# A prologue rebuilt: the long convolution on x as it lies in memory, and weights split in place

## The chip, the cores and the metric

The program runs on one NeuronCore of a Trainium2 chip. The metric is the device time of one execution in microseconds. Three runs of the kernel before took 577.61, 577.98 and 578.83 us (median 577.98). TensorE does the matrix products, VectorE and ScalarE (DVE and ACT in the profile) the elementwise work, GpSimd (POOL) a third share of it; SyncE (SP) issues all the transfers, which run on 16 DMA engines.

## The reference

Two stages on x, of shape (64 batches, 32 channels, 512 positions), float32. The first is a long convolution per channel whose taps are computed from parameters, cut off at each batch's length:

```python
kernel = _get_kernel(log_dt, C, log_A_real, A_imag, Lq)     # (32, 512): a sum over 64 complex modes
y = irfft(rfft(u * mask) * rfft(kernel))[..., :Lq]          # causal convolution along the positions
y = (y + u * mask * D[:, None]) * mask                      # mask: position < length of the batch
x = x + y
```

The second is a gated network on rows of 512, with 64 batches x 32 channels = 2048 rows, an inner size of 1376, and a low-rank addition (rank 16, one of 16 tables chosen by the batch's index) on each of its three products:

```python
gate = x @ W_gate.T + 0.5 * (x @ A_gate[i].T) @ B_gate[i].T
up   = x @ W_up.T   + 0.5 * (x @ A_up[i].T)   @ B_up[i].T
act  = silu(gate) * up
x = x + act @ W_down.T + 0.5 * (act @ A_down[i].T) @ B_down[i].T
```

## The kernel before

The kernel has a prologue (the convolution, and the splitting of the weights) and then 16 tiles of 128 rows for the gated network. Every engine runs a list of instructions of its own, and the order is written out by hand: only semaphores tie the engines together, so an instruction that waits holds back everything behind it on its engine. That holds for SP too, whose list is the order in which transfers are issued.

*The tiles* (`body` on each engine) take each product as three passes in a short float32 form: a value is split into a high part (ScalarE copies it into the short form) and a low part (value less high part), and high*high, high*low and low*high are summed. A tile needs `w_hi`, `w_lo` (gate and up weights, in 12 pieces: 3 chunks of columns x 4 blocks of rows) and `wd_hi`, `wd_lo` (down weights, 6 pieces).

*The splitting of the weights.* SP loads a piece into one of three staging slots (`load_piece`, L226), ScalarE writes its high part (`split_hi`, L445), GpSimd subtracts to get the low part (`split_lo`, L393) and so frees the slot. The last down pieces are split during tile 0.

*The taps.* VectorE works out the parameters in a long chain of small dependent steps (L612 to L722, 128x32 values each), of which GpSimd turns one result into the exponents of all magnitudes (L407) and ScalarE takes their exponential in one instruction (L469). Then, for each of four groups of 8 channels, VectorE reduces phases (L645 to L656), ScalarE takes sines (L452 to L456), VectorE builds two tables (L739 to L747), TensorE multiplies them (L924, `taps`) and VectorE copies the result out (L727, L728). SP writes these taps to `kpad` in DRAM (`store_taps`, L239), where each channel has 128 zeros and then its 512 taps.

*The convolution* goes by 16 pairs of channels. x lies in SBUF with the position within a block of 128 on the partitions. For each pair SP reads from `kpad` a matrix `toep` of 128 rows x 2 channels x 512 values (`load_toep`, L247), in which row p is the row of taps that starts p+1 values into the channel. Rows that start later as p grows fit an input whose positions are reversed, and so each pair of x is also loaded a second time, reversed by the host: `um` from `xr` (`load_um`, L252). VectorE masks `um` (L755), TensorE does 8 products into PSUM (`conv`, L937), VectorE masks the result into `cv` (L759), and adds it to x (L765; GpSimd for the first four pairs, L400). There are four slots of `toep` and `um` (RC = 4); the load for pair p waits until pair p-4 has been convolved. After the last pair VectorE gathers the first tile's columns of x into `xt` (L810), TensorE starts the low-rank product on them (L967), the high and the low part of `xt` are made, and tile 0 begins.

The transfer on which `toep` rests reads, with one instruction, with these steps and counts (slowest first, in values of 4 bytes):

```python
src = bass.AP(tensor=kpad, offset=pair * (2 * (P + NL)) + 1, ap=[[1, P], [P + NL, 2], [1, NL]])
```

Of the kernel before, what the change touches and what calls it, by code (L numbers as in the profile page):

```python
# [14 lines left out]
F32 = mybir.dt.float32  # L15
# [5 lines left out]
P = 128  # L21
# [18 lines left out]
RS = 3  # L40
# [21 lines left out]
def program(nc, xT, xr, wgu, wd, atab, btab, prm, lens, idx, out):  # L62
    top = ExitStack()
    with top:
# [6 lines left out]
        kpad = nc.dram_tensor("kpad", (NH, P + NL), F32, kind="Internal")  # L71


        w_hi = sb(top, "w_hi", [P, KB, WG], F32R)
        w_lo = sb(top, "w_lo", [P, KB, WG], F32R)
        x = sb(top, "x", [P, NH, KB, NB])
        ident = sb(top, "ident", [P, P])
        amask = sb(top, "amask", [P, NH, BT])
# [4 lines left out]
        with ExitStack() as pk:  # L83
# [7 lines left out]
            prm_sb = sb(pk, "prm_sb", [P, N_PRM, NH])  # L91
# [3 lines left out]
            zeros = sb(pk, "zeros", [NH, P])  # L95
            k_sb = sb(pk, "k_sb", [PA, NG, HG, PB])

        wd_hi = sb(top, "wd_hi", [P, FB, NL + LR], F32R)
        wd_lo = sb(top, "wd_lo", [P, FB, NL + LR], F32R)
# [4 lines left out]
        b_raw = [sb(top, "b_raw0", [LR, 2 * 512])]  # L104


        with ExitStack() as pa:
            toep = sb(pa, "toep", [P, RC, 2, NL])
            um = sb(pa, "um", [P, RC, 2 * KB * NB])
            cv = sb(pa, "cv", [P, 2, 2 * KB * NB])  # L110
            len_i = sb(pa, "len_i", [P, NB], I32)
            len_f = sb(pa, "len_f", [P, NB])
            lcol = sb(pa, "lcol", [P, 2, KB])
            lmask = sb(pa, "lmask", [P, 2, KB, NB])
            stage = sb(pa, "stage", [P, RS, 2 * 512])


        b_raw.append(sb(top, "b_raw1", [LR, 2 * 512]))
# [5 lines left out]
        x_lo = sb(top, "x_lo", [P, 2, KB, P], F32R)  # L124
        h_act = sb(top, "h_act", [P, 2, 512])
# [22 lines left out]
        stage_in = [sem(f"stage_in{i}") for i in range(RS)]  # L148
        stage_hi, stage_lo = sem("stage_hi"), sem("stage_lo")
        consts, ident_s, amask_ok, amask_ps, amaskt_ok = (sem("consts"), sem("ident_s"), sem("amask_ok"), sem("amask_ps"),  # L150
                                                 sem("amaskt_ok"))
# [3 lines left out]
        logmag, mag_done, trig_in, trig_done = sem("logmag"), sem("mag_done"), sem("trig_in"), sem("trig_done")  # L155
# [4 lines left out]
        um_in = [sem(f"um_in{i}") for i in range(RC)]  # L160
        um_ready, conv_ps, conv_sb, x1_pool = sem("um_ready"), sem("conv_ps"), sem("conv_sb"), sem("x1_pool")
        x1_dve = sem("x1_dve")
# [38 lines left out]
        for c in range(NC):  # L201
            for kb in range(KB):
                cols = slice(chunk_col(c, 0), chunk_col(c, 0) + 2 * CH[c][1])
                pieces.append((wgu[kb * P:(kb + 1) * P, cols], w_hi[:, kb, cols], w_lo[:, kb, cols], P, (2 * CH[c][1],)))
        for f0 in range(0, FB - 1, 2):
            pieces.append((wd[f0 * P:(f0 + 2) * P, :].rearrange("(g p) n -> p g n", p=P),
                           wd_hi[:, f0:f0 + 2, 0:NL], wd_lo[:, f0:f0 + 2, 0:NL], P, (2, NL)))
        pieces.append((wd[(FB - 1) * P:NF, :], wd_hi[0:FLAST, FB - 1, 0:NL], wd_lo[0:FLAST, FB - 1, 0:NL], FLAST, (NL,)))

        NP_GU = KB * NC  # L210

        def staged(n):
            shape = pieces[n][4]
            size = shape[0] * (shape[1] if len(shape) > 1 else 1)
            v = stage[0:pieces[n][3], n % RS, 0:size]
            return v.rearrange("p (g n) -> p g n", g=2) if len(shape) > 1 else v
# [6 lines left out]
        def _(sp):  # L223
# [25 lines left out]
            def load_um(pair, slot, first):  # L249
                if not first:  # L250
                    sp.wait_ge(conv_ps, pair - RC + 1)
# [889 lines left out]
```

## Time and profile before

| | us |
|---|---|
| median of three runs | 577.98 |
| the profiled execution | 577.4 |
| its span, from the first to the last instruction | 575.5 |
| TensorE busy in the span | 518.0 |
| first product of pair 0 of the convolution | 45.23 |
| first product of tile 0 (low-rank, L967) | 101.66 |
| granted clock of TensorE over the span | 0.99 |

Times in the profile count from the start of the span. A group of instructions is named by line, engine, operation and the tensors it writes and reads; "x16" is the number of instructions. An idle time is put down to whatever ended it. In a window, the DMA share is the mean busy share of the 16 DMA engines (a little over 1 where packets overlap), and GB/s is what they moved together.

### The profile page before, as it was taken

The page shows a single profiled execution, that of the slowest core. Times are in us where ns is not written, and L with a number is a line of the kernel's source. Part 1 is how long each engine was busy: PE and PEld are TensorE (multiplying, and loading weights), DVE is VectorE, ACT ScalarE, POOL GpSimd, SP SyncE. Part 2 cuts the span into 40 slices and gives each one's busy share as a digit, 9 for nine tenths or more (in the row PEclk, how much of TensorE's full clock was granted, in tenths as well). Part 3 has the DMA queues.
Part 4 walks back from the last instruction along what each step waited for, and adds up shares of the span by engine and source line. Part 5 has one row for each costly group of instructions (what it writes and reads, how often), then busy time and mean ns, then how long its engine had stood idle before and what let it go on. Part 6 is the DMA issues. An engine that isn't in the chain of part 4 may idle for free.

```text
span 575.5 us, 10131 instructions
## 1 busy us (share of the span) xinstructions
PE 518.0 (90%) x3169; PEld 475.4 (83%) x3169; DVE 297.7 (52%) x577; ACT 194.3 (34%) x394; POOL 74.2 (13%) x74
## 2 busy tenths in 40 slices
PE   0007897999999999999999999999999999999997
PEld 0006887798989898989999999999999999998987
DVE  7989768874444444444353535353535353535342
ACT  3613101743333333333333324242423333333331
POOL 7434412640000000000000000000000000000000
PEclk9999999899999999999999999999999999999999
DMA  7626898730404040404040403030303030303000
GB/s 286 235 55 203 288 324 291 180 103 23 113 5 115 2 119 0 120 0 119 0 115 5 114 6 110 10 110 10 107 13 107 13 107 13 107 13 107 14 19 19
DMA packets 32307, 53.20 MB, mean 92 GB/s; under 512 B 7586, under 2 KB 16194, under 8 KB 32290
## 3 DMA queue, kind: packets, MB, share of 16 engines
q1 hardware_dynamic: 32290, 53.00, 31.3%
q8 instruction: 8, 0.13, 0.1%
q14 instruction: 9, 0.07, 0.1%
HBM read 48.69 MB, written 4.28 MB: 92 GB/s over the span
## 4 chain that ended last, share of the span: by engine, by line
PE 85%; DVE 11%; DMA 1%; issue 1%; POOL 1%; ACT 0%; DVEq 0%; SPq 0%; ACTq 0%
PE ps_u L989 21%; PE ps_g L989 20%; PE ps_db L1025 12%; PE ps_da L1025 12%; PE ps_x L1016 3%; PE ps_x L967 2%; PE ps_u L937 2%; PE ps_g L999 2%; PE ps_g L1000 2%; PE ps_u L1000 2%; PE ps_u L999 2%; PE ps_g L937 2%; PE ps_x L1054 1%; DMA um<-xr 1%; PE ps_da L1083 1%
## 5 line engine op out<-in xcount | busy, mean ns | idle before, releaser
L825 DVE TENSOR_TENSOR b_spl<-b_raw,b_spl 64x512 fp32r<-64x512 f32 (+1 forms) x96 | 66.6, 695 | 52.5 <-ACT b_spl L499 49.0
L499 ACT CAST b_spl<-b_raw 64x512 fp32r<-64x512 f32 (+1 forms) x96 | 54.6, 569 | 76.8 <-PE ps_u L1000 76.8
L989 PE MATMUL ps_g<-w_hi,x_hi 128*128 128x512 f32 (+1 forms) x192 | 72.8, 379 | 0.0
L989 PE MATMUL ps_g<-w_lo,x_hi 128*128 128x512 f32 (+1 forms) x192 | 71.1, 370 | 0.0
L989 PE MATMUL ps_g<-w_hi,x_lo 128*128 128x512 f32 (+1 forms) x192 | 71.0, 370 | 0.0
L989 PE MATMUL ps_u<-w_lo,x_hi 128*128 128x512 f32 (+1 forms) x192 | 70.7, 368 | 0.0
L989 PE MATMUL ps_u<-w_hi,x_hi 128*128 128x512 f32 (+1 forms) x192 | 70.6, 368 | 0.0
L989 PE MATMUL ps_u<-w_hi,x_lo 128*128 128x512 f32 (+1 forms) x192 | 70.5, 367 | 0.0
L434 POOL COPY xt<-x 128x512 f32 (+1 forms) x15 | 9.8, 653 | 394.5 <-PE ps_x L1054 390.9
L861 DVE TENSOR_TENSOR h_act<-h_act,ps_u 128x512 f32<-128x512 f32 (+1 forms) x48 | 30.4, 633 | 52.2 <-PE ps_u L1000 52.1
L1025 PE MATMUL ps_da<-wd_hi,ht_hi 128*128 128x288 f32 (+1 forms) x176 | 54.6, 310 | 0.0
L1025 PE MATMUL ps_db<-wd_hi,ht_hi 128*128 128x288 f32 (+1 forms) x176 | 53.2, 302 | 0.0
L1025 PE MATMUL ps_db<-wd_hi,ht_lo 128*128 128x288 f32 (+1 forms) x176 | 52.0, 296 | 0.0
L1025 PE MATMUL ps_db<-wd_lo,ht_hi 128*128 128x288 f32 (+1 forms) x176 | 51.9, 295 | 0.0
L1025 PE MATMUL ps_da<-wd_lo,ht_hi 128*128 128x288 f32 (+1 forms) x176 | 51.8, 294 | 0.0
L1025 PE MATMUL ps_da<-wd_hi,ht_lo 128*128 128x288 f32 (+1 forms) x176 | 51.7, 294 | 0.0
L518 ACT ACTIVATE h_act<-ps_g 128x512 f32<-128x512 f32 (+1 forms) x48 | 26.5, 552 | 63.9 <-PE ps_g L1000 63.9
L868 DVE TENSOR_TENSOR ht_lo<-ps_x,ht_hi 128x512 fp32r<-128x512 f32 (+1 forms) x48 | 28.9, 603 | 30.0 <-ACT ht_hi L534 28.3
L989 PEld LDWEIGHTS ps_g<-w_hi,x_lo 128*128 128x128 f32 x192 | 36.4, 189 | 5.4
L989 PEld LDWEIGHTS ps_u<-w_hi,x_hi 128*128 128x128 f32 x192 | 36.1, 188 | 5.2
L989 PEld LDWEIGHTS ps_u<-w_hi,x_lo 128*128 128x128 f32 x192 | 36.0, 188 | 5.1
L989 PEld LDWEIGHTS ps_u<-w_lo,x_hi 128*128 128x128 f32 x192 | 36.0, 188 | 5.1
(167 smaller groups left out, 986.6 us busy)
## 6 DMA issues: line engine op xcount, KB each, us to landing
a_raw<-atab SPq DMA_DIRECT2D x64, 152.0 KB, 2.4
toep<-kpad SPq DMA_DIRECT2D x16, 512.0 KB, 5.4
b_raw<-btab SPq DMA_DIRECT2D x128, 64.0 KB, 2.1
stage<-wgu SPq DMA_DIRECT2D x8, 512.0 KB, 5.0
um<-xr SPq DMA_DIRECT2D x16, 256.0 KB, 5.7
x<-xT SPq DMA_DIRECT2D x8, 512.0 KB, 6.7
out<-y_sb SPq DMA_DIRECT2D x15, 256.0 KB, 2.1
b_raw<-btab SPq DMA_DIRECT2D x64, 44.0 KB, 1.8
```

The lines of the kernel that those rows point to most:

```text
L499: nc.scalar.copy(b_spl[0:LR, up, 0:w], b_raw[slot][:, up * w:(up + 1) * w]).then_inc(b_hi, 1)
L518: nc.scalar.activation(h_act[:, s, 0:w], ps_g[s][:, 0:w], ACT.Silu).then_inc(silu_ok, 1)
L825: V.tensor_tensor(b_spl[LR:P, up, 0:w], b_raw[slot][:, up * w:(up + 1) * w], b_spl[0:LR, up, 0:w].bitcast(F32), ALU.subtract).then_inc(b_l ...
L861: V.tensor_tensor(h_act[:, s, 0:w], h_act[:, s, 0:w], ps_u[s][:, 0:w], ALU.mult).then_inc(act_ok, 1)
L868: V.tensor_tensor(ht_lo[:, f0:f0 + full, :], ps_x[bank][:, 0:full * P].rearrange("p (f t) -> p f t", t=P), ht_hi[:, f0:f0 + full, :].bitca ...
L937: last = T.matmul(ps_c[slot][:, at + d * NB:at + KB * NB], toep[:, slot, h, d * P:(d + 1) * P], um[:, slot, at:at + n], start=(d == 0), st ...
L967: ins = T.matmul(ps_x[0][:, 0:P], w, xt[:, kb, :], start=(kb == 0), stop=(kb == KB - 1))
L989: T.matmul(ps[:, 0:w], xs[:, q, kb, :], ws[:, kb, col:col + w], start=(kb == 0 and xs is x_hi and ws is w_hi), stop=False)
L999: T.matmul(ps[:, 0:w], t_hi[:, up, :], b_spl[:, up, 0:w], start=False, stop=False)
L1000: T.matmul(ps[:, 0:w], t_lo[:, up, :], b_spl[:, up, 0:w], start=False, stop=True).then_inc(u_ps if up else g_ps, 1)
L1016: ins = T.transpose(ps_x[bank][0:rows, f * P:(f + 1) * P], h_act[:, s, f * P:f * P + rows], ident[:, :])
L1025: ins = T.matmul(ps[:, 0:c1 - c0], hs[0:rows, f, :], ws[0:rows, f, c0:c1], start=(f == 0 and hs is ht_hi and ws is wd_hi), stop=(bank == 1 ...
```

## The change

- The convolution reads x as it lies. `um`, `xr`, `cv` and the masks on the input are gone. The rows of `toep` now start one value *earlier* as p grows, so the source of the load steps backwards. `kpad` holds two copies of all taps, each written by its own transfer; rows 0 to 63 of `toep` are read from the first copy and rows 64 to 127 from the second. So the source of a load has, slowest first, a step from one copy to the other (count 2), a step back by one value (count 64) and the 512 values of a row. A pair is loaded by two transfers, one for each channel.
- 1 is added to tap 0 besides D, so that the product is x plus the convolution, and one predicated copy per pair (`copy_predicated`, where the position is below the length) writes it from PSUM over x. VectorE does all 16 pairs. The input needs no mask, since the convolution is causal.
- Weights are loaded with no staging slots, straight to where their low part will be (`w_raw` and `w_lo` are the same memory). ScalarE writes the high part (`top_part`); the low part is subtracted in place (`rem_part`): gate and up pieces 0 to 7 by GpSimd, which begins only when all four tables are built (`tab_ready`), pieces 8 to 11 by VectorE behind pairs 10 to 13, and the 6 down pieces by VectorE in tile 0.
- SP issues all of x and then all 12 gate and up pieces before the first taps are stored. The down pieces go out one at a time behind the `toep` loads of pairs 10 to 15, and the first tile's low-rank tables behind those of pairs 8 and 9.
- The magnitudes are computed on ScalarE, 32 instructions of 128x48 with the exponent's factor as scale, in place of GpSimd's four and ScalarE's one.
- `take_x` gathers the first tile in two steps, the second for the last four channels only. `amask` is smaller; its transposed form is made before the convolution.

The core of the diff ("..." marks what is left out):

```diff
-        kpad = nc.dram_tensor("kpad", (NH, P + NL), F32, kind="Internal")
+        kpad = nc.dram_tensor("kpad", (2, NH, P + NL), F32, kind="Internal")
...
             def load_piece(n):
-                wait(sp, stage_lo, n - RS + 1)
-                sp.dma_start(staged(n), pieces[n][0]).then_inc(stage_in[n % RS], 16)
+                sp.dma_start(pieces[n][1], pieces[n][0]).then_inc(w_in[n], 16)
...
                 sp.wait_ge(k_ready, g + 1)
-                dst = bass.AP(tensor=kpad, offset=g * HG * (P + NL) + P, ap=[[PB, PA], [P + NL, HG], [1, PB]])
-                sp.dma_start(dst, k_sb[:, g, :, :]).then_inc(k_out[g], 16)
+                for i in range(2):
+                    dst = bass.AP(tensor=kpad, offset=(i * NH + g * HG) * (P + NL) + P,
+                                  ap=[[PB, PA], [P + NL, HG], [1, PB]])
+                    sp.dma_start(dst, k_sb[:, g, :, :]).then_inc(k_out[g], 16)
 
             def load_toep(pair, slot, group, first):
 
-                sp.wait_ge(k_out[group], 16)
+                sp.wait_ge(k_out[group], 32)
                 if not first:
                     sp.wait_ge(conv_ps, pair - RC + 1)
-                src = bass.AP(tensor=kpad, offset=pair * (2 * (P + NL)) + 1, ap=[[1, P], [P + NL, 2], [1, NL]])
-                sp.dma_start(toep[:, slot, :, :], src).then_inc(toep_in[slot], 16)
...
+                for h in range(2):
+                    src = bass.AP(tensor=kpad, offset=(2 * pair + h) * (P + NL) + P,
+                                  ap=[[NH * (P + NL) - P // 2, 2], [-1, P // 2], [1, NL]])
+                    sp.dma_start(toep[:, slot, h, :], src).then_inc(toep_in[slot], 16)
...
+            for g in range(NG):
+                load_x(g, 0)
+                load_x(g, 1)
+            for n in range(NP_GU):
+                load_piece(n)
...
+            sp.wait_ge(zero_out, 32)
             store_taps(0)
             for pair in range(RC):
                 load_toep(pair, pair, 0, True)
             store_taps(1)
+            load_toep(RC, 0, 1, False)
             store_taps(2)
+            load_toep(RC + 1, 1, 1, False)
+            store_taps(3)
+            load_toep(RC + 2, 2, 1, False)
+            load_toep(RC + 3, 3, 1, False)
...
+            for pair in range(2 * RC, PAIRS):
+                load_toep(pair, pair % RC, pair // RC, False)
+                if pair == 2 * RC:
+                    load_a(0, 0, ids0)
+                if pair == 2 * RC + 1:
+                    load_b(0, 0, 0, ids0)
+                if pair >= 2 * RC + 2:
+                    load_piece(NP_GU + pair - (2 * RC + 2))
...
+            def rem_part(n):
+                pool.wait_ge(w_top, n + 1)
+                nc.gpsimd.tensor_tensor(pieces[n][3], pieces[n][1], pieces[n][2].bitcast(F32),
+                                        ALU.subtract).then_inc(w_rem_pool, 1)
...
+            pool.wait_ge(tab_ready, 2 * NG)
+            for n in range(KB):
+                rem_part(n)
             pool.wait_ge(a_in, 16 * BT)
             pack_a(0)
-            for n in range(10, len(pieces)):
-                split_lo(n)
+            for n in range(KB, NP_POOL):
+                rem_part(n)
...
+            def magnitudes(g):
+                for h in range(g * HG, (g + 1) * HG):
+                    ins = nc.scalar.activation(gg[:, g, h - g * HG, :], lvec[:, :], ACT.Exp, scale=small[:, DAR, h:h + 1])
+                ins.then_inc(mag_done, 1)
...
-            def mask_output(pair, slot):
+            def add_conv(pair):
+
                 dve.wait_ge(conv_ps, pair + 1)
-                V.tensor_tensor(two(cv[:, slot % 2, :]), two(ps_c[slot][:, :]), mask_out, ALU.mult).then_inc(conv_sb, 1)
...
+                V.copy_predicated(x[:, 2 * pair:2 * pair + 2, :, :].rearrange("p h k b -> p h (k b)"),
+                                  lmask[:, :, :].rearrange("p k b -> p (k b)").unsqueeze(1).broadcast_to([P, 2, KB * NB]),
+                                  ps_c[pair % RC][:, :].rearrange("p (h n) -> p h n", h=2)).then_inc(x1_ok, 1)
...
             taps(3)
...
+            for pair in range(1, PAIRS - 2):
+                add_conv(pair)
+                if pair >= PAIRS - 6:
+                    rem_part(NP_POOL + pair - (PAIRS - 6))
+            dve.wait_ge(x1_ok, PAIRS - 2)
+            take_x(0, NH - 4).then_inc(xt_ok, 1)
+            add_conv(PAIRS - 2)
+            add_conv(PAIRS - 1)
+            dve.wait_ge(x1_ok, PAIRS)
+            take_x(NH - 4, NH).then_inc(xt_ok, 1)
...
+            def conv(pair):
+                slot = pair % RC
+                pe.wait_ge(toep_in[slot], 32 * (pair // RC) + 32)
+                pe.wait_ge(x_in[2 * pair // HG], 32)
+                wait(pe, x1_ok, pair - RC + 1)
```

TensorE's order is as before: taps(0), conv(0), taps(1), conv(1) to conv(3), taps(2), conv(4), taps(3), and then the other pairs.

## Rows read from the trace of the kernel before

**Rows 1.** The page: busy time by engine, and the chain's shares.

```profile
PE 518.0 (90%) x3169; PEld 475.4 (83%) x3169; DVE 297.7 (52%) x577; ACT 194.3 (34%) x394; POOL 74.2 (13%) x74
...
PE 85%; DVE 11%; DMA 1%; issue 1%; POOL 1%; ACT 0%; DVEq 0%; SPq 0%; ACTq 0%
```

**Rows 2.** Timeline of PE: start us, us, what [idle before <- who ended it].

```profile
45.23 4.95 PE L937 MATMUL ps_g<-um,toep 128*128 128x256 f32 x16 [6.92 <-DMA toep<-kpad]
77.42 4.98 PE L937 MATMUL ps_g<-um,toep 128*128 128x256 f32 x32
92.30 5.00 PE L937 MATMUL ps_u<-um,toep 128*128 128x256 f32 x32 [0.21 <-issue]
101.66 2.08 PE L967 MATMUL ps_x<-xt,a_gu 128*128 128x128 f32 x8 [4.17 <-DVE amask_t L813]
107.89 0.50 PE L999 MATMUL ps_g<-b_spl,t_hi 128*128 128x512 f32 x1 [0.27 <-DVE t_lo L851]
```

**Rows 3.** Timeline of VectorE, the chain of parameters.

```profile
5.38 3.64 DVE L620 SCALAR_TENSOR_TENSOR small<-small 128x64 f32<-128x64 f32 x6
10.84 0.80 DVE L678 TENSOR_SCALAR small<-small 128x32 f32<-128x32 f32 x1
14.02 2.32 DVE L682 SCALAR_TENSOR_TENSOR small<-small 128x32 f32<-128x32 f32 x1
26.79 2.29 DVE L714 TENSOR_TENSOR small<-prm_sb,small 128x32 f32<-128x32 f32 x1
33.71 0.19 DVE L717 TENSOR_TENSOR small<-prm_sb,small 128x32 f32<-128x32 f32 x1
38.66 0.16 DVE L728 TENSOR_TENSOR k_sb<-k_sb,prm_sb 1x8 f32<-1x8 f32 x1
```

**Rows 4.** Timeline of GpSimd.

```profile
26.68 6.94 POOL L393 TENSOR_TENSOR w_lo<-stage,w_hi 128x1024 fp32r<-128x1024 f32 x3 [7.68 <-ACT w_hi L445]
```

**Rows 5.** Windows: PE, PEld, DVE, ACT, POOL busy, granted clock, DMA share, GB/s.

```profile
0.00:5.00 5.00, 0.00 (x0) 0.00 (x0) 2.15 (x8) 1.28 (x1) 3.49 (x17) 1.00 0.59 169
5.00:10.00 5.00, 0.00 (x0) 0.00 (x0) 4.66 (x13) 2.36 (x3) 2.70 (x2) 1.00 0.76 293
8.00:20.00 12.00, 0.00 (x0) 0.00 (x0) 11.90 (x23) 1.93 (x2) 10.30 (x7) 1.00 1.02 392
75.00:95.00 20.00, 19.79 (x130) 18.83 (x131) 15.62 (x26) 0.00 (x0) 0.00 (x0) 1.00 1.01 337
```

**Rows 6.** The `toep` loads by their line: time to landing.

```profile
L247 SPq DMA_DIRECT2D toep<-kpad x16: 370/377/593, 40.4 to 87.3; - x16
...
DMA to landing us min/median/max: 4.0/5.4/8.9
```

**Rows 7.** The stores of taps by their line.

```profile
L239 SPq DMA_DIRECT2D kpad<-k_sb x4: 337/387/432, 38.9 to 70.7; - x4
...
DMA to landing us min/median/max: 1.5/2.7/4.6
```

**Rows 8.** VectorE by line, 60 to 101 us: count | busy, mean ns.

```profile
L755 DVE TENSOR_TENSOR um<-um,lmask 128x512 f32<-128x512 f32 x12 | 8.3, 690 | 5.9 <-DMA um<-xr 5.9
L759 DVE TENSOR_TENSOR cv<-ps_u,lmask 128x512 f32<-128x512 f32 x8 | 5.4, 680 | 0.0
L765 DVE TENSOR_TENSOR x<-x,cv 128x512 f32<-128x512 f32 x4 | 3.7, 920 | 0.1
L810 DVE COPY xt<-x 128x512 f32<-128x512 f32 x1 | 1.8, 1774 | 0.0
```

**Rows 9.** Timelines of ScalarE (sine, high parts) and VectorE (low parts).

```profile
20.42 0.23 ACT L464 ACTIVATE small<-small 128x32 f32<-128x32 f32 x1
101.66 0.62 ACT L491 CAST x_hi<-xt 128x512 fp32r<-128x512 f32 x1 [3.22 <-DVE xt L810]
103.04 1.29 DVE L825 TENSOR_TENSOR b_spl<-b_raw,b_spl 64x512 fp32r<-64x512 f32 x2
105.32 0.30 ACT L508 CAST t_hi<-t_m 64x128 fp32r<-64x128 f32 x1
```

More of the change, by code:

```diff
@@ L39 @@
 DB_W = NL - DA_W
-RS = 3
 RC = 4
@@ L94, in program @@
             half_pi = sb(pk, "half_pi", [P, 1])
-            zeros = sb(pk, "zeros", [NH, P])
-            k_sb = sb(pk, "k_sb", [PA, NG, HG, PB])
         wd_hi = sb(top, "wd_hi", [P, FB, NL + LR], F32R)
+        with ExitStack() as landing:
+            wd_raw = sb(landing, "wd_raw", [P, FB, NL + LR])
         wd_lo = sb(top, "wd_lo", [P, FB, NL + LR], F32R)
@@ L124, in program @@
         x_lo = sb(top, "x_lo", [P, 2, KB, P], F32R)
+        with ExitStack() as pa:
+            with ExitStack() as pz:
+                zeros = sb(pz, "zeros", [NH, P])
+            toep = sb(pa, "toep", [P, RC, 2, NL])
+            len_i = sb(pa, "len_i", [P, NB], I32)
+            len_f = sb(pa, "len_f", [P, NB])
+            lcol = sb(pa, "lcol", [P, KB])
+            lmask = sb(pa, "lmask", [P, KB, NB], I32)
+            prm_sb = sb(pa, "prm_sb", [P, N_PRM, NH])
+            k_sb = sb(pa, "k_sb", [PA, NG, HG, PB])
         h_act = sb(top, "h_act", [P, 2, 512])
@@ L396, in add_conv @@
-            def add_conv(pair):
-                pool.wait_ge(conv_sb, pair + 1)
-                v = x[:, 2 * pair:2 * pair + 2, :, :].rearrange("p h k b -> p (h k b)")
-                nc.gpsimd.tensor_tensor(v, v, cv[:, pair % 2, :], ALU.add).then_inc(x1_pool, 1)
-            split_lo(0)
-            pool.wait_ge(consts, 6)
-            pool.wait_ge(dar_ok, 1)
-            for g in range(NG):
-                shape = [P, HG, PA + PB]
-                nc.gpsimd.tensor_tensor(gg[:, g], small[:, DAR, g * HG:(g + 1) * HG].unsqueeze(2).broadcast_to(shape),
-                                        lvec[:, :].unsqueeze(1).broadcast_to(shape), ALU.mult).then_inc(logmag, 1)
@@ L457, in trig @@
                                      scale=-1.0).then_inc(trig_done, 1)
-            for n in range(RS):
-                split_hi(n)
-            act.wait_ge(consts, 6)
+            act.wait_ge(amask_ok, 5)
+            nc.scalar.copy(amask_w[:, :, :], amask[0:LR, :].unsqueeze(1).broadcast_to([LR, NH, BT])).then_inc(amaskw_ok, 1)
+            act.wait_ge(consts, 5)
             act.wait_ge(ang_in, 1)
@@ L521, in ht_hi_part @@
                     act.wait_ge(ht_ps, NC * t + c + 1)
-                    if c == 0 and first:
-                        act.wait_ge(stage_lo, len(pieces))
-                    elif c == 0:
-                        act.wait_ge(down_ps, t)
+                    if c == 0:
+                        wait(act, down_ps, t)
                     f0, nf = BLK[c]
@@ L579, in _ @@
             b_hi_part(0, 0, 0, 1)
-            split_hi(NP_GU)
             tiles(act, body)
```

298 lines of the change are left out of this document (93 added, 205 removed).

## The prediction

> **What bounds the kernel now.** I read the page first: TensorE is busy for 518.0 of 575.5 us and has 85% of the chain that ended last, VectorE 11% [rows 1]. The timeline of TensorE says where the rest lies. Tile 0 starts at 101.66 and from 107.89 on the products run with no gap, so the tiles are bound by TensorE, and nothing of the change touches tiles 1 to 15. What the change can move is the point at which the first L999 runs, 107.89 [rows 2]. Everything before it is a chain of three parts:
>
> 1. VectorE's parameters, up to the first taps at 38.66 + 0.16 = 38.8 [rows 3].
> 2. Store and load: pair 0's product starts at 45.23, after TensorE has idled 6.92 us for `toep` [rows 2].
> 3. Sixteen pairs, 45.23 to 97.3. At full clock a pair takes 4.98 / 2 = 2.49 us, a first one after idling 4.95 [rows 2]. Then the tail, 97.3 to 107.89: 10.6 us.
>
> **Part 1, the parameters: -15.6 us.** VectorE's small operations take about 0.2 us (L717: 0.19) [rows 3], but 2.3 us where GpSimd is splitting weights: L714 starts at 26.79 and takes 2.29, within GpSimd's three subtractions from 26.68 to 33.62 [rows 3, 4]. So one operation of VectorE waits for one of GpSimd's, each time. The change leaves GpSimd idle until all tables are built. What goes: L620's six, 3.64 - 6 x 0.24 = 2.2; beside GpSimd's exponents L678 to L680 and L645, four times 0.80 - 0.18 = 2.5; L682 and L684, 2 x 2.1 = 4.3; L714 to L716, 3 x 2.1 = 6.3; of the lost mask instructions about 0.3. Sum 15.6, first taps at 23.2. The magnitudes on ScalarE are 32 instructions, each between 0.13 (starts apart) and 0.23 us (L464) [rows 9], 4 to 7 us in all, of which tables(0) needs 8: hidden beside VectorE's 9 us from the sines to table 0. Without that cover they would cost 2 us.
>
> **Part 2, what now lies ahead of the first store.** SP issues 0.1 MB of parameters, 4.19 MB of x and 5.64 MB of weights before it. The first ten microseconds moved 5 x 169 + 5 x 293 = 2.3 MB, and after that 392 GB/s are reached [rows 5]: the remaining 7.6 MB take 19.4 us, to 29.4. The store is issued at 23.3 and lands behind them, about 31.5 (the landing is 1.5 to 4.6 us when a queue is short [rows 7]), so 6 of the 15.6 us are given back. The first `toep` load is at the engines at 32.5. Doubled store and zeros cost 0.4 us of SP each and are in this.
>
> **Part 3, the loads of `toep`, the term that decides.** No row of before shows such a transfer. All bulk loads of before count 32 or more in the slowest step on both sides (`toep`: 128 rows). The new source counts 2 in its slowest step, then 64 backwards; the two halves can't be joined into one step. If the 16 engines get equal parts of the slowest step, only two parts can be given out. The bounds:
>
> - Below: a full-width load, 4.0 us to land, 5.4 in the median [rows 6]. Two loads a pair cost SP 0.37 us more, hidden in 2.49.
> - Above: two engines do all of it. In the stretch at 392 GB/s and share 1.02 one engine moves 392 / 16 / 1.02 = 24.0 GB/s; in the stretch of `toep` loads 337 / 16 / 1.01 = 20.9 [rows 5]. A load of 256 KB is 131,072 bytes an engine, 5.46 us at 24.0, and a pair takes 10.9 us instead of 2.49.
>
> I take the upper end and 24.0: a second copy of the taps makes sense only if the slowest step is the copy, and then this step is what a transfer is cut along; the other 14 engines would not be there to crowd the same rows of DRAM, which speaks for 24.0 and against 20.9.
>
> The Trainium skill says it outright (DMA: Bandwidth & Descriptors, section Why a DMA increments its semaphore by 16 and not by 1): a transfer issued by SP runs on the largest number of engines up to 16 that divides the count of the slowest step on both sides, here 2. No run here shows it yet. By the same page's 27 GiB/s an engine a pair would take 9.0 us, and the time would be some 670, an estimate.
>
> The sum for the upper end: four pairs of loads from 32.5, 43.7 us, to 76.2. The second store of taps (issued at about 50) has its share on the two busy engines and lands only behind them, so the fifth load is issued late: 2.5 us. Twelve pairs, 131.0 us, to 209.7. In between, the two engines also carry a sixteenth each of 3.5 MB (first tables and five down pieces), 0.22 MB, 9.1 us: to 218.8. Stores 3 and 4 find loads queued and add nothing. Pair 15's product runs on a TensorE that has idled, 4.95 us [rows 2]: the convolution ends at 223.8, where before it was 97.3.
>
> **Masks and adds.** Three passes of 0.68 to 0.92 us a pair (L755, L759, L765) become one predicated copy [rows 8]. Its price is not in the trace: between 0.68 and the three it replaces, 2.3. I take 0.7. Both ends are under 2.49 us a pair, so this is worth nothing until the last pair.
>
> **Weights.** The 18 high parts stay on ScalarE, with nothing behind them that is due. GpSimd's eight subtractions (6.94 / 3 = 2.3 us each [rows 4]) begin after table 3 and end before the last pair in either case. Four on VectorE behind pairs 10 to 13, about 0.9 us each (two inputs in SBUF, 704 long, by L765's 0.68 at 512), fit in a pair's 2.49. In tile 0, six take VectorE 1.3 us at most; they stand ahead of low parts that TensorE needs 6 and 12 us after 107.89, with 2 us to spare, and GpSimd no longer holds VectorE there. Nothing either way; without that slack, up to 2 us. The x loads that now all come first feed conv with no wait.
>
> **The tail: -3.7 us.** Before, from 97.3, the last mask (0.68), the last add and the gather run, the last two held up by GpSimd (1.77 for the gather, and the add's mean is 0.92 against 0.68 undisturbed [rows 8]); the low-rank product starts at 101.66. After: predicated copy 0.7, small gather 0.3, `x_hi` 0.62, `x_lo` 0.69, two low parts 1.29, the mask's copy 0.21 and t_m 0.29, four `t_hi` at 0.31 and four `t_lo` at 0.30 [rows 9], waits 0.4: 6.9 instead of 10.6. The last down piece lands before it.
>
> **The sum.** First L999 at 223.8 + 6.9 = 230.7, which is 122.8 later than 107.89. The profiled execution took 577.4 us (span 575.5), which becomes 700.2; the median of the runs stands 0.6 above that execution, so 701. By the bounds of the engine's rate: at 20.9 the loads and the rest take 27 more, 728; at 26 (the same share at the best) 14 less, 687. Start of the loads, bubbles and landings between pairs may be off by 10 either way, and a latency of 1 us exposed in each of 16 pairs would add 16. Own range 665 to 745.
>
> **The rivals.**
>
> - *Full width after all.* If the engines are dealt the rows whatever the outermost count is, pair 0 starts at 32.5 + 4.0 = 36.5, 8.7 us earlier. Then 16 pairs as before, about 52 us: the first is cold (4.95), pairs 5 and 6 wait for stores 3 and 4, which SP has ahead of their loads; from pair 10 on, 1.05 MB a pair at 337 GB/s take 3.1 us and slip by 1.5 in all behind four slots. End 90, tail 6.9: L999 at 96.9, 11 us earlier, time 566 to 567, within 556 to 574. For it: every load of before lands in 4.0 to 8.9 us [rows 6]. Against it: none of them had this shape. This is the rival on the other side; it decides where the last pair ends before 97.3 + 3.7 = 101.0, so where a pair's loads take less than (101.0 - 4.95 - 2.5 - 32.5) / 16 = 3.8 us, which is 138 GB/s, or between five and six engines at 24.0.
> - *Partial width.* A cut over four engines (say, over both steps in part) gives 5.46 us a pair: 32.5 + 87.4 + 2.5 + 4.6 + 2.5 + 6.9 = 136.4, 28.5 later, 606.
> - *Full width, but late landings.* Loads that land at 8.9 instead of 4.0 us [rows 6] for the three that TensorE waits for in the open (pairs 0, 5, 6) cost 14.7, and pairs 10 to 15 at 3.1 us another 4: 566.5 + 18.7 = 585, slower by 7.
>
> **How the numbers follow.** Two engines 0.77, full width 0.16, four engines or so 0.04, late landings 0.03. The predicted time is the first's, 701. Its own range of 665 to 745 holds 0.75, so the range goes down to the third case, 604 to 745. A measurement of this kernel can tell 0.2% from no change. Faster: the second case, 0.17 with what late landings leave; within 0.2%: 0.02; slower 0.81.
>
> **What the profile would show.** First `k_sb` sum at 23 us instead of 38.7, no VectorE operation of 2.3 us before it; pair 0's product at 43 to 46 in the narrow case (36 to 38 in the wide one), then TensorE idle until `toep` lands in most pairs, starts 10 to 12 us apart; DMA share near 2/16 and about 50 GB/s between 40 and 210 us; in TensorE's clock a long cold stretch; the tiles unchanged behind it. `toep` loads landing in 4 to 6 us with TensorE dense from 37 us on would prove me wrong at once, and so would a DMA share near 1 in that stretch.

## The result: 22% slower, and the profile after

The changed kernel takes 703.11 us (median of four runs, 703.03 to 703.19) against 578.11 us (four runs, 577.61 to 578.83): 1.2167 times as long, 95% interval 1.2145 to 1.2189. 701 us had been forecast. The profiled execution took 703.17 us, its span is 701.0.

The page after: busy time, two rows of the 40 slices of the span (TensorE's granted clock in tenths, and what the DMA engines moved), and the chain's shares.

```profile
PE 551.4 (79%) x3169; PEld 499.9 (71%) x3169; DVE 257.0 (37%) x556; ACT 200.4 (29%) x426; POOL 39.5 (6%) x55
...
PEclk9995556655567999999999999999999999999999
...
GB/s 315 266 47 51 41 52 50 92 76 101 75 90 39 81 12 100 41 59 88 10 98 31 67 87 11 98 22 76 81 17 97 16 84 77 22 95 12 89 15 16
...
PE 68%; SPq 19%; DMA 7%; DVE 3%; issue 1%; ACT 0%; DVEq 0%
```

TensorE had 85% of the chain [rows 1] and has 68%; SP's queue, absent before, has 19%. From the third slice (35 us on) 315 GB/s have become about 50, and 75 to 101 in the slices from 123 us on, where tables and down pieces are loaded beside `toep`. From the fourth slice to the twelfth (53 to 210 us) the clock stands at 0.5 to 0.6, near its lower level of 1.2 GHz. TensorE's product count is the same; it is busy 33 us longer, mostly since a pair's products take up to 4.96 us at the lower clock, against 2.49 [rows 2].

The timeline of TensorE: start, duration, what, and in brackets the idle time before it and who ended it.

```profile
44.21 4.51 PE L866 MATMUL ps_g<-x,toep 128*128 128x256 f32 x16 [22.07 <-DMA toep<-kpad]
55.32 4.08 PE L866 MATMUL ps_g<-x,toep 128*128 128x256 f32 x16 [5.99 <-DMA toep<-kpad]
65.75 4.96 PE L866 MATMUL ps_u<-x,toep 128*128 128x256 f32 x16 [6.35 <-DMA toep<-kpad]
76.22 4.96 PE L866 MATMUL ps_u<-x,toep 128*128 128x256 f32 x16 [5.51 <-DMA toep<-kpad]
90.35 4.95 PE L866 MATMUL ps_g<-x,toep 128*128 128x256 f32 x16 [8.21 <-DMA toep<-kpad]
...
205.16 4.26 PE L866 MATMUL ps_u<-x,toep 128*128 128x256 f32 x16 [7.19 <-DMA toep<-kpad]
217.81 4.75 PE L866 MATMUL ps_u<-x,toep 128*128 128x256 f32 x16 [8.39 <-DMA toep<-kpad]
...
229.31 0.50 PE L924 MATMUL ps_g<-b_spl,t_hi 128*128 128x512 f32 x1 [1.22 <-DVE t_lo L769]
```

Read the starts: 44.21, 55.32, 65.75, 76.22. A pair comes every 10.5 us, and each time TensorE has been idle for a `toep` load. L924 answers to L999 of before [rows 2] and starts at 229.31 instead of 107.89: 121.4 us later. The span grew by 125.5. So 121.4 us of the loss lie ahead of this row, and 4.1 behind it.

The windows (engines' busy time, granted clock, DMA share, GB/s) show the loads:

```profile
8.00:20.00 12.00, 0.00 (x0) 0.00 (x0) 10.87 (x58) 10.45 (x33) 0.00 (x0) 1.00 1.03 413
20.00:30.00 10.00, 1.04 (x16) 0.93 (x16) 8.39 (x21) 7.49 (x17) 0.00 (x0) 1.00 0.92 351
40.00:45.00 5.00, 0.79 (x2) 0.70 (x3) 0.00 (x0) 0.00 (x0) 0.00 (x0) 1.00 0.13 51
45.00:80.00 35.00, 17.15 (x76) 15.38 (x75) 5.37 (x14) 8.65 (x12) 0.00 (x0) 0.64 0.13 47
```

A share of 0.13 is 2 of 16 engines. A pair is 524,288 bytes, 262,144 for each of two engines, in 10.5 us: 25.0 GB/s an engine. The row of before for the stretch in which `toep` is loaded has share 1.01 and 337 GB/s [rows 5].

VectorE's first steps and its last ones ahead of tile 0, and the timeline of SP's queue:

```profile
4.50 1.52 DVE L563 SCALAR_TENSOR_TENSOR small<-small 128x64 f32<-128x64 f32 x6
16.98 0.19 DVE L656 TENSOR_TENSOR small<-prm_sb,small 128x32 f32<-128x32 f32 x1
22.49 0.16 DVE L670 SCALAR_TENSOR_TENSOR k_sb<-k_sb,prm_sb 1x8 f32<-1x8 f32 x1
...
222.59 0.72 DVE L696 COPY_PREDICATED x<-lmask,ps_u 128x512 f32<-128x512 int32 x1 [12.41 <-PE ps_u L866]
223.35 0.19 DVE L706 COPY xt<-x 128x64 f32<-128x64 f32 x1
```

```profile
22.73 0.84 SPq L235 DMA_DIRECT2D kpad<-k_sb  x2
30.29 31.89 SPq L245 DMA_DIRECT2D toep<-kpad  x8
62.22 6.29 SPq L235 DMA_DIRECT2D kpad<-k_sb  x2
```

The first taps are there at 22.65 (before 38.8 [rows 3]), and L563's six take 1.52 instead of 3.64. The store is issued at once, but the first `toep` load only at 30.29. Before, 1.6 us lay between taps and load (38.8 to 40.4 [rows 3, 6]), now 7.6: of the 16 us won, 6 are given back behind the weights.

### The profile page after: what moved, and what is told of

It is laid out like the page before. It is cut to its first block, busy times and chain, and to the rows that moved or that the text cites. A ratio compares the mean times of both kernels' runs of the same rounds, so it can differ in the third digit from the quotient of the medians.

```text
span 701.0 us, 10101 instructions
## 1 busy us (share of the span) xinstructions
PE 551.4 (79%) x3169; PEld 499.9 (71%) x3169; DVE 257.0 (37%) x556; ACT 200.4 (29%) x426; POOL 39.5 (6%) x55
## 4 chain that ended last, share of the span: by engine, by line
PE 68%; SPq 19%; DMA 7%; DVE 3%; issue 1%; ACT 0%; DVEq 0%
PE ps_u L914 17%; PE ps_g L914 17%; SPq L245 13%; PE ps_db L952 10%; PE ps_da L952 10%; DMA toep<-kpad 5%; SPq L220 4%; PE ps_x L943 3%; DMA kpad<-k_sb 2%; PE ps_x L893 2%; PE ps_g L924 1%; PE ps_u L924 1%; PE ps_u L925 1%; PE ps_g L925 1%; PE ps_x L981 1%; SPq L257 1%
## 5 line engine op out<-in xcount | busy, mean ns | idle before, releaser
L866 PE MATMUL ps_g<-x,toep 128*128 128x256 f32 (+3 forms) x128 | 37.5, 482 | 69.7 <-DMA toep<-kpad 69.7
L866 PEld LDWEIGHTS ps_g<-x,toep 128*128 128x128 f32 x128 | 33.4, 316 | 73.5 <-DMA toep<-kpad 70.7
L743 DVE TENSOR_TENSOR b_spl<-b_raw,b_spl 64x512 fp32r<-64x512 f32 (+1 forms) x96 | 60.4, 630 | 53.1 <-ACT b_spl L454 49.4
L866 PE MATMUL ps_u<-x,toep 128*128 128x256 f32 (+3 forms) x128 | 38.3, 489 | 52.5 <-DMA toep<-kpad 52.5
L866 PEld LDWEIGHTS ps_u<-x,toep 128*128 128x128 f32 x128 | 34.1, 322 | 56.7 <-DMA toep<-kpad 53.9
L952 PE MATMUL ps_da<-wd_hi,ht_hi 128*128 128x288 f32 (+1 forms) x176 | 54.6, 310 | 0.0
L952 PE MATMUL ps_db<-wd_hi,ht_hi 128*128 128x288 f32 (+1 forms) x176 | 53.3, 303 | 0.0
L952 PE MATMUL ps_db<-wd_lo,ht_hi 128*128 128x288 f32 (+1 forms) x176 | 52.0, 295 | 0.0
L952 PE MATMUL ps_db<-wd_hi,ht_lo 128*128 128x288 f32 (+1 forms) x176 | 51.9, 295 | 0.0
L952 PE MATMUL ps_da<-wd_lo,ht_hi 128*128 128x288 f32 (+1 forms) x176 | 51.8, 294 | 0.0
L952 PE MATMUL ps_da<-wd_hi,ht_lo 128*128 128x288 f32 (+1 forms) x176 | 51.6, 293 | 0.0
L398 ACT CAST wd_hi<-wd_raw 128x1024 fp32r<-128x1024 f32 (+1 forms) x6 | 5.8, 973 | 151.6 <-DMA wd_raw<-wd 151.6
```

The lines of the kernel that those rows point to most:

```text
L743: V.tensor_tensor(b_spl[LR:P, up, 0:w], b_raw[slot][:, up * w:(up + 1) * w], b_spl[0:LR, up, 0:w].bitcast(F32), ALU.subtract).then_inc(b_l ...
L866: last = T.matmul(ps_c[slot][:, at + d * NB:at + KB * NB], toep[:, slot, h, d * P:(d + 1) * P], v, start=(d == 0), stop=(d == KB - 1))
L952: ins = T.matmul(ps[:, 0:c1 - c0], hs[0:rows, f, :], ws[0:rows, f, c0:c1], start=(f == 0 and hs is ht_hi and ws is wd_hi), stop=(bank == 1 ...
```

## The experiments

**How wide is a load?** The theory on test is that the slowest step of the source, with count 2, is what a transfer is cut along. Then 4, 8 and 16 copies of the taps give 4, 8 and 16 engines. All three start from the changed kernel. The edit for 4:

```diff
-        kpad = nc.dram_tensor("kpad", (2, NH, P + NL), F32, kind="Internal")
+        kpad = nc.dram_tensor("kpad", (4, NH, P + NL), F32, kind="Internal")
...
-                for i in range(2):
+                for i in range(4):
...
-                                  ap=[[NH * (P + NL) - P // 2, 2], [-1, P // 2], [1, NL]])
+                                  ap=[[NH * (P + NL) - P // 4, 4], [-1, P // 4], [1, NL]])
```

Four copies:

> Four copies of the taps instead of two, so that the slowest step of a load's source counts 4 (32 rows backwards in each); two more stores a group. Theory of width (a load runs on as many engines as that count, 25 GB/s each): 512 KB on 4 engines is 5.2 us a pair instead of 10.5, DMA share about 0.25 in the stretch of the loads, time about 610 us. Rival theory of issue (SP spends 3.6 to 6.6 us on the issue of each backwards load, and that sets the pace): a pair still takes 10 us or more, time 701 to 710. Rival theory of backwards rows (DRAM or engines are slow when rows go down): no change either, 701 to 710.

Eight copies:

> Eight copies: the slowest step counts 8, eight stores a group. Width: 2.6 us a pair, about what TensorE takes (2.49); first store 2.4 us later, two later stores exposed by as much; time about 571 (564 to 582). Issue or backwards rows: 705 or more.

Sixteen copies:

> Sixteen copies: the slowest step counts 16, sixteen stores a group of 0.4 us of SP each. Width: loads of 256 KB land in 4 to 5 us, TensorE paces the pairs, but each group's store holds SP for 6.4 us, three of them in the open; time about 581 (572 to 592). Issue or backwards rows: 710 or more.

Measured: 630.82 us with four copies (ratio to the kernel before 1.0926, interval 1.0878 to 1.0975), 600.63 with eight (1.0404, 1.0362 to 1.0445), 601.49 with sixteen (1.0419, 1.0368 to 1.0469). One window of each (last two columns: share and GB/s), first four copies while little but `toep` is loaded, with two starts from TensorE's timeline:

```profile
41.00:60.00 19.00, 14.04 (x74) 12.78 (x75) 5.38 (x14) 8.65 (x12) 0.00 (x0) 0.93 0.26 88
```

```profile
51.57 2.62 PE L866 MATMUL ps_u<-x,toep 128*128 128x256 f32 x16 [1.94 <-DMA toep<-kpad]
57.10 4.29 PE L866 MATMUL ps_u<-x,toep 128*128 128x256 f32 x16 [2.91 <-DMA toep<-kpad]
```

Then eight copies, while nothing but `toep` is loaded, and sixteen, beside the down pieces, with the first store in SP's queue:

```profile
40.00:46.00 6.00, 4.65 (x16) 4.29 (x16) 0.00 (x0) 0.00 (x0) 0.00 (x0) 1.00 0.52 201
```

```profile
95.00:115.00 20.00, 14.51 (x94) 13.39 (x92) 8.23 (x12) 4.18 (x4) 8.02 (x4) 1.00 1.06 269
```

```profile
26.11 13.62 SPq L235 DMA_DIRECT2D kpad<-k_sb  x16
```

Share 0.13 with two copies, 0.26 with four, 0.52 with eight, 1.06 with sixteen: the width is the count of copies. With four, 5.5 us lie between the two pairs above, where it was 10.5.

All three times missed my numbers on the slow side, by 20 to 30 us. Two reasons hold for all of them. The first is the stores: SP issues every copy of every group by itself, 13.62 us for the first sixteen (9.40 for the first eight), with the loads queued behind, so that pair 0 starts at 46.33 with sixteen copies and 41.35 with eight, against 44.21 with two, and the later groups' stores stand ahead of loads too. The second is the down pieces, which take their part of the same engines: beside them the late pairs were 7 us apart with four copies, where I had taken 5.2, and 4.8 us with eight, where I had taken 2.6. With sixteen copies the rate comes on top: all engines are busy (1.06) but move 269 GB/s where the kernel before moves 337 [rows 5]. Eight copies show no such loss, with 201 / 16 / 0.52 = 24 GB/s an engine. So more copies recovered most of the loss, and none of the three kernels recovered all of it.

**Is it the 269 GB/s of an unlucky distance between the copies?** Copies of 81,920 bytes, an even distance; one spare channel makes it 84,480.

```diff
-        kpad = nc.dram_tensor("kpad", (16, NH, P + NL), F32, kind="Internal")
+        kpad = nc.dram_tensor("kpad", (16, NH + 1, P + NL), F32, kind="Internal")
```

> c16_sixteen_copies with each copy of the taps 2,560 bytes further on in DRAM (pitch 84,480 instead of 81,920 bytes). There 16 engines at a share of 1.05 moved only 268 GB/s, where the kernel before moved 337 at 1.01. If the pitch of the copies makes the engines meet in DRAM: above 320 GB/s at the same share and a time 5 us or more lower, about 595. If it is the cut of the rows over the engines (eight neighbouring rows each) or the step backwards: 260 to 275 GB/s and 600 to 602.

Measured: 599.55 us in a single run, and 251 GB/s at share 0.93 from 95 to 118 us. Divided by its share, that is 270 GB/s; by the same measure it is 254 at the even distance (269 / 1.06) and 334 in the kernel before (337 / 1.01). The distance is not what costs the most of it.

**Is it the width alone, or going backwards, or the rest of the rebuild?** The kernel before, with forward sources as ever, gets two copies and two loads a pair, once with the slowest step of 2, once with 128 rows as the slowest step:

```diff
-                src = bass.AP(tensor=kpad, offset=pair * (2 * (P + NL)) + 1, ap=[[1, P], [P + NL, 2], [1, NL]])
-                sp.dma_start(toep[:, slot, :, :], src).then_inc(toep_in[slot], 16)
+                for h in range(2):
+                    src = bass.AP(tensor=kpad, offset=(2 * pair + h) * (P + NL) + 1,
+                                  ap=[[NH * (P + NL) + P // 2, 2], [1, P // 2], [1, NL]])
+                    sp.dma_start(toep[:, slot, h, :], src).then_inc(toep_in[slot], 16)
```

In the control, the middle of the three reads `ap=[[1, P], [1, NL]]`, and all else is the same. The narrow one:

> The kernel before with one thing changed: two copies of the taps, two loads a pair, each with a source of 2 x 64 rows x 512 that goes forwards. Width: the rebuilt prologue has no part in it, a pair takes 10.5 us plus the two engines' share of the reversed x and the weights, and the time goes to about 716 (700 to 735). Backwards rows: forwards is what it was, 578 to 584. Issue (if it is the backwards step that makes the issue slow): 578 to 584 as well.

The control:

> Control for b2: the kernel before with two copies stored and two loads a pair, as there, but each load with 128 rows in its slowest step (from the first copy alone). Width: all that b2 lost comes back, 578 to 583 (two more stores, 16 more loads on SP, the last two behind nothing). If it was the doubling of stores and loads that cost b2 its 140 us: 700 or more.

Measured: 718.34 us narrow (ratio 1.2442, 1.2392 to 1.2493), 578.19 for the control (1.0004, 0.9979 to 1.0028). TensorE in the narrow one, and a window of the control:

```profile
65.97 4.80 PE L942 MATMUL ps_g<-um,toep 128*128 128x256 f32 x16 [5.05 <-DMA toep<-kpad]
77.55 4.14 PE L942 MATMUL ps_u<-um,toep 128*128 128x256 f32 x16 [6.79 <-DMA toep<-kpad]
```

```profile
75.00:95.00 20.00, 19.71 (x132) 18.77 (x131) 15.06 (x25) 0.00 (x0) 0.00 (x0) 1.00 0.96 331
```

11.6 us a pair in the old kernel, read forwards. This is the cleanest of the comparisons: the two differ in one access pattern, and the whole loss is there. It needs no backwards step and nothing of the rebuild, and two copies with two transfers a pair cost nothing by themselves.

A third variant of the kernel before asks why sixteen copies move only 269 GB/s; it reads forwards with `[NH * (P + NL) + P // 16, 16], [1, P // 16]`:

> The kernel before with sixteen copies of the taps, two loads a pair, each load of 16 x 8 rows x 512 forwards, eight neighbouring rows an engine. It tells apart why c16_sixteen_copies moved only 268 GB/s at a DMA share of 1.05. If it is the cut (eight neighbouring rows an engine): the stretch of the last eight pairs moves 260 to 290 GB/s at a share near 1, and a packet of 2 KB takes about 126 ns in the mean. If it is the step backwards: 330 GB/s or more there, as in the kernel before (337 at 1.01, 100 ns a packet). Sixteen stores a group cost about 6 us of SP each, three of them in the open, so the time is 590 to 610 either way.

Measured: 613.27 us in a single run. The last 15 us in which `toep` is loaded:

```profile
115.00:130.00 15.00, 14.12 (x88) 13.20 (x88) 9.04 (x15) 0.00 (x0) 0.00 (x0) 0.97 1.07 286
```

286 GB/s at share 1.07 are 267 by the measure above, with single stretches of 5 us between 263 and 320 GB/s. The mean lies in the range that was written down for the cut (260 to 290). A packet of 2,048 bytes (`toep` and `um` together) took 125.2 ns in the mean of this stretch, against 99.7 in the kernel before (75 to 95 us) and 126.5 with sixteen copies read backwards (95 to 115 us). That is what the cut was expected to show, too. So the direction is not what lowers the rate. It is the cut into 16 groups of 8 neighbouring rows, or the reading from 16 copies that comes with it; these two were not separated, and why they cost is open.

**Could SP's issue be the limit?** In the trace after, SP's queue is held for long at each load. By this line's summary (least, median, most, in ns) against 370/377/593 [rows 6]:

```profile
L245 SPq DMA_DIRECT2D toep<-kpad x32: 497/3620/6566, 30.3 to 197.5; - x32
```

If issuing were the limit, a second issuer would help. The loads of the odd channels go to ScalarE:

```diff
+            def load_second(pair):
+                slot = pair % RC
+                act.wait_ge(k_out[pair // RC], 32)
+                if pair >= RC:
+                    act.wait_ge(conv_ps, pair - RC + 1)
...
+                act.dma_start(toep[:, slot, 1, :], src).then_inc(toep_in[slot], 16)
```

> The changed kernel, with the load of each pair's second channel issued by ScalarE instead of SP; shapes as they are (slowest step counts 2). Width: both issuers give their loads to the same two engines, a pair takes 10.5 us as before, DMA share stays at 0.13, time 695 to 705. Issue (SP's 3.6 to 6.6 us a load are its own work, not a wait for the two engines): a pair takes 5.3 us, time about 620.

Measured: 700.51 us (ratio 1.2100, 1.2031 to 1.2170), where the changed kernel has 1.2167. The window from 55 to 77 us:

```profile
55.00:77.00 22.00, 11.04 (x35) 9.77 (x36) 1.15 (x4) 1.21 (x4) 0.00 (x0) 0.50 0.14 48
```

Still two engines, still 48 GB/s, from two queues. The 3.6 us in SP's queue are back-pressure, an effect and not the cause.

**What is the rest of the change worth?** The changed kernel with the old, forward load of a full pair. It needs the reversed input, so `um` is loaded again, but not masked; everything else of the change stays. Its queue order: four pieces ahead of the first store, the others among the loads.

```diff
+                src = bass.AP(tensor=kpad, offset=pair * (2 * (P + NL)) + 1, ap=[[1, P], [P + NL, 2], [1, NL]])
+                sp.dma_start(toep[:, slot, :, :], src).then_inc(toep_in[slot], 16)
+                if not first:
+                    load_um(pair)
```

> The rest of the change with the loads of the kernel before: one copy of the taps, one load a pair with 128 rows forwards, and x a second time with positions reversed as TensorE's input, unmasked; the predicated copy, the weights in place, the magnitudes and the tail as in the change; loads of weights spread over the convolution. If the width of the loads is all that is wrong with the change: first taps at 22.7, pair 0 at about 29.5, pairs as before (50 to 52 us), tail 6.8 us: first L999-like product at 88, time about 558 (552 to 566). If the predicated copy, the late low parts or the tail cost something that the narrow loads hid: 570 or more.

Measured: 574.05 us (ratio 0.9899, 0.9847 to 0.9950); I had expected 558. In the profiled execution, the slowest of the four at 575.96 us, pair 0 starts at 28.24, 17 us earlier than before, yet the first L938 (L999 of before) only at 101.71. Three windows show where the lead went:

```profile
50.00:55.00 5.00, 1.82 (x7) 1.61 (x6) 4.80 (x6) 0.00 (x0) 4.74 (x3) 0.50 0.27 29
60.00:65.00 5.00, 5.00 (x35) 4.72 (x33) 1.47 (x2) 1.56 (x2) 0.00 (x0) 1.00 1.05 374
80.00:85.00 5.00, 3.94 (x26) 3.54 (x25) 2.12 (x4) 2.09 (x2) 0.00 (x0) 1.00 1.05 387
```

The engines stand nearly idle at 50 us (29 GB/s), while SP waits to store taps that don't exist yet with loads queued behind, and from 60 us on they are full. If the DMA engines are the bound of the prologue once the parameters are short, a hole in their work is paid for at the end.

So the same kernel with its queue filled: the pieces that fit go ahead of the stores that wait, and four down pieces (not in these lines) go behind all `toep` loads.

```diff
             store_taps(1)
-            load_piece(6)
             load_toep(RC, 0, 1, False)
-            load_piece(7)
+            load_piece(6)
             load_toep(RC + 1, 1, 1, False)
-            store_taps(2)
+            load_piece(7)
             load_piece(8)
             load_toep(RC + 2, 2, 1, False)
-            store_taps(3)
             load_piece(9)
+            store_taps(2)
             load_toep(RC + 3, 3, 1, False)
             load_piece(10)
+            load_piece(11)
+            store_taps(3)
```

> hk_forward_loads with another order of transfers: pieces 6 to 11 issued ahead of stores 2 and 3, so that the engines have work while SP waits for taps, and only two down pieces ahead of the last pair, the other four behind it, split in tile 0 as in the kernel before. If the bytes ahead of the last pair bound hk_forward_loads (its engines stood at 0.27 of their time in 50 to 55 us and at 1.05 from 60 to 85): 2 MB less there and no hole, about 10 us earlier, 562 (557 to 568). If it is the chain of waits from store 3 to pair 7: 570 to 574.

Measured: 563.64 us (ratio 0.9757, 0.9713 to 0.9801), as expected (562). From 50 to 85 us, and the row that sets the start of the dense part:

```profile
50.00:85.00 35.00, 29.95 (x176) 27.87 (x175) 12.35 (x19) 5.83 (x8) 14.28 (x7) 0.91 1.00 331
```

```profile
89.34 0.50 PE L947 MATMUL ps_g<-b_spl,t_hi 128*128 128x512 f32 x1 [1.22 <-DVE t_lo L792]
```

No hole is left, and the tiles become dense at 89.34 instead of 101.71 (107.89 in the kernel before). Two things changed together, though. The four down pieces that went behind the loads are 1.77 MB, some 5 us at the 374 GB/s above (an estimate), and the rest of the 12.4 us is what filling the hole is worth. The two were not run one by one. The time lies where the bytes ahead of the last pair had put it, and clear of the 570 to 574 of a chain of waits.

**Does it matter that GpSimd waits for the tables?** In the kernel with forward loads, that one wait is gone:

```diff
-            pool.wait_ge(tab_ready, 2 * NG)
```

> As hk_forward_loads, but GpSimd subtracts as soon as a high part is there and does not wait for the tables. If GpSimd's subtractions hold VectorE by up to 2.3 us each, as they did in the kernel before, tables 1 to 3 come later and with them pairs 4 to 8: 2 to 6 us slower than hk_forward_loads, with VectorE operations of 2.3 us in its trace. If VectorE has slack there: the same within 1 us.

Measured: 577.02 us (ratio 0.9984, 0.9959 to 1.0009), 3.0 us slower than with the wait, within what was expected. The size is less sure than the sign: the four runs with the wait spread from 571.06 to 575.96 us, and the two profiled executions differ by 0.5. VectorE's last step of the first taps, and its second product of table 1, without the wait:

```profile
22.48 0.16 DVE L681 SCALAR_TENSOR_TENSOR k_sb<-k_sb,prm_sb 1x8 f32<-1x8 f32 x1
31.35 2.58 DVE L699 TENSOR_TENSOR e<-e,small 128x256 f32<-128x256 f32 x1
```

The same product with the wait:

```profile
29.15 0.42 DVE L700 TENSOR_TENSOR e<-e,small 128x256 f32<-128x256 f32 x1
```

GpSimd was subtracting from 28.79 to 38.6 in the first, and taps(1) came at 39.14 instead of 33.12. So the wait keeps table 1 short. It is not what shortened the parameters: the first taps are there at 22.64 without it too, because a subtraction needs a high part, and ScalarE writes its first one only at 27.66, behind the sines and the magnitudes. In the kernel before, GpSimd already subtracted at 6.59, 13.54 and 26.68 and raised the magnitudes' exponents from 9.65, in the middle of VectorE's chain.

**Why do the tiles take longer?** The 4 us behind L924 are in no step of the prediction. The tiles' period can be read from one row per tile, the low-rank product. Tile 1's and tile 15's are 14 periods apart. The changed kernel:

```profile
252.18 1.05 PE L893 MATMUL ps_x<-xt,a_gu 128*128 128x128 f32 x8
...
664.06 1.05 PE L893 MATMUL ps_x<-xt,a_gu 128*128 128x128 f32 x8
```

The kernel before, tile 1 and tile 11, ten periods:

```profile
130.52 1.05 PE L967 MATMUL ps_x<-xt,a_gu 128*128 128x128 f32 x8
...
422.36 1.05 PE L967 MATMUL ps_x<-xt,a_gu 128*128 128x128 f32 x8
```

411.88 / 14 = 29.42 us against 291.84 / 10 = 29.18. The kernels with eight copies and with the filled queue, both made from the changed one, have 29.42 too; the control made from the kernel before has 29.2. The difference is in the products of 512 columns. Here are the first and the twelfth of a row of twelve in tile 1, changed kernel first:

```profile
258.84 0.40 PE L914 MATMUL ps_u<-w_hi,x_hi 128*128 128x512 f32 x1
...
261.41 0.40 PE L914 MATMUL ps_u<-w_hi,x_lo 128*128 128x512 f32 x1
```

```profile
137.13 0.39 PE L989 MATMUL ps_u<-w_hi,x_hi 128*128 128x512 f32 x1
...
139.62 0.39 PE L989 MATMUL ps_u<-w_hi,x_lo 128*128 128x512 f32 x1
```

Eleven steps take 2.57 us against 2.49. In the mean of all 16 tiles one step takes 0.233 us against 0.228, and a tile has 48 of these products: 0.005 x 48 = 0.24 us, the whole difference of the period.

TensorE's instructions in a tile are the same. What differs is where the tensors lie: `amask` shrank from 512 bytes a partition to 16, beside a new `amask_w` of 512, and all that is allocated behind them (`x_hi`, `x_lo`, `b_spl`, `wd` and so on, but not `w_hi` and `w_lo`) sits 32 bytes further on. By the declarations, with the 16 bytes rounded up to 32, that is 32 more than a multiple of 64 where before it was a multiple of 64; no trace prints the addresses. In the kernel with the filled queue, one declaration moves to the end, which gives all these tensors the addresses of before:

```diff
-        amask = sb(top, "amask", [P, BT])
         amask_w = sb(top, "amask_w", [LR, NH, BT])
...
         ht_lo = sb(top, "ht_lo", [P, FB, P], F32R)
+        amask = sb(top, "amask", [P, BT])
```

> The kernel of the filled queue (563.64 us, ratio 0.9757, span 561.7), with one declaration moved: in all rebuilt kernels the mask tensor `amask` takes 16 bytes a partition where the kernel before gives it 512, beside `amask_w` of 512, and every tensor allocated behind it (wd, a_gu, b_spl, x_hi, x_lo, t_hi, ht_hi and so on) lies 32 bytes off the 64-byte boundary that it had before. Here `amask` is declared last, so that all tensors of the tiles lie at exactly the addresses of the kernel before; not one instruction differs. The question is the one step of the prediction that failed, the tiles unchanged: a tile takes 29.42 us in the changed kernel and all its relatives, 29.2 in the kernel before and in the two kernels built on it, and a 512-column product starts 0.233 us after the one before it against 0.227. Theory A, addresses: the tile's period goes back to 29.2, the products to 0.227, and the time falls by 15 to 16 tiles x 0.23 = 3.5 us, to 560 (559 to 561.5), ratio 0.969. Theory B, not the addresses (the instruction stream itself, since the tiles' operations in place or on another engine differ): the period stays at 29.42 and the time at 563 to 564.5, ratio 0.975. A value between says that both play a part.

Measured: 560.81 us (five runs, 559.08 to 561.68; ratio 0.9697, 0.9671 to 0.9723), and the period:

```profile
112.29 1.05 PE L916 MATMUL ps_x<-xt,a_gu 128*128 128x128 f32 x8
...
521.01 1.05 PE L916 MATMUL ps_x<-xt,a_gu 128*128 128x128 f32 x8
```

408.72 / 14 = 29.19. The steps between the products are back at 0.228 us in the mean. The period shows the effect more sharply than the two times do, since their intervals overlap. It was the addresses: not one instruction differs between these two kernels. Which tensor's it was is not separated. This version beats both kernels: 17 us less than before, by 18.3 us in the prologue (first L947 at 89.58) less 1.5 behind it.

## Why the prediction was right, and its one wrong step

- **The width of the loads** decided everything, and it was as forecast: two engines, by share 0.13, at 25.0 GB/s an engine (24.0 taken), a pair in 10.5 us alone (10.9) and 12.2 beside the down pieces (156.75 to 217.81 over five pairs). The long stretch at the lower clock came with it, as nine of the 40 slices show. The Trainium skill's rule (DMA: Bandwidth & Descriptors, section Why a DMA increments its semaphore by 16 and not by 1) gives a transfer of SP the largest number of engines up to 16 that divides the slowest count on both sides. The traces agree at 2, 4, 8 and 16 (shares 0.13, 0.26, 0.52, 1.06).
- **The parameters**: taps at 22.65, forecast 23.2. L563 to L670 show no 2-us holds. The reason given was half right: VectorE is free because GpSimd is idle, but it is not the wait for the tables that idles it here. Without that wait the first taps come at 22.64 as well, and the holds return only in table 1. By the traces it is that the exponents left GpSimd and that ScalarE's high parts come later; no run separates the two.
- **What lies ahead of the first store**: pair 0 at 44.21, forecast 32.5 + 10.9 = 43.4. That close a hit is in part luck. The first load was issued at 30.29, earlier than the 32.5 taken (DMA moved 413 GB/s from 8 to 20 us, 392 taken), and pair 0 then took 13.9 us and not 10.9. From 30 to 32 us the engines moved 6 GB/s; what held the first load is open.
- **The second store behind the narrow loads**: forecast 2.5 us. Pair 4 came 14.13 us after pair 3, 3.6 more than 10.5.
- **Predicated copy**: 0.72, forecast 0.7. **Tail**: from 222.56, where pair 15's product ends, to 229.31, 6.75 us, forecast 6.9; before it was 10.6. L924 at 229.31, forecast 230.7.
- **The wrong step: "nothing of the change touches tiles 1 to 15".** They took 0.24 us more each, 3.3 us over 14 periods; the rest of the 4 us lies in tile 0 (0.2) and the last 37 us (0.5) and was not followed. It was argued from TensorE's instruction list alone, and the size of one mask moved the addresses under it. The error of the sum, 701 against 703.1, hides it: the prologue came 1.4 us earlier than forecast, the tiles 4.1 later.
- **The full-width rival** had been priced at 566 to 567 us. It was never run as it stood. The nearest kernel to it came out at 574.05 with a queue order of its own, and 563.64 with another. So SP's order is worth some 10 us once the loads are wide, and the price had no term for it.
- **The rival of four engines** had 606. Four copies took 630.8, since SP's stores and the down pieces' share came on top.

## What to carry to other kernels

Before a source's access pattern is changed, read off the count of its slowest step: here it set how many DMA engines carried the transfer, and with 2 there a load of 524 KB took 10.5 us instead of being hidden. Here it was the reversed input, one more transfer a pair, that was the cheap half of the trade: kept, with the rest of the change around it, the queue reordered and the addresses restored, it gave 560.8 us instead of 703.1. When a change shrinks or moves a tensor on chip, compare the period of the untouched loop before and after: a shift of 32 bytes took 0.8% of this one.

## What had not been expected of the hardware

- A narrow transfer holds the issuing queue: 3.62 us in the median and up to 6.57 for each load on SP, against 0.38 for the wide ones. With four copies the median is 1.16 us, with sixteen 0.59.
- Sixteen groups of 8 neighbouring rows, each from a copy of its own, ran all engines (share 1.06) at 269 GB/s where 128 rows as the slowest step gave 337 in the kernel before and 331 at share 0.96 in its control with two loads a pair. Read forwards it is little better (286 at 1.07, with `um` loaded beside it). Why is open.
- With the tensors behind `amask` shifted by 32 bytes, a product of 512 columns took 0.005 us longer (0.233 against 0.228 from start to start), though its operand of 512 columns, `w_hi` or `w_lo`, had not moved. The down products kept their mean durations (L952 against L1025: 303 and 302 ns for `wd_hi,ht_hi` into `ps_db`, 295 and 295 for `wd_lo,ht_hi`).
